# Scan's beginning for block 0, moved from the scan stage into the mixture's results

## What is computed

```python
# L1_ffn: two of 16 experts for each token, and a shared one
score = sigmoid(x @ gate_w + gate_b); top two, their scores scaled to a sum of 1
y = mlp(x, shared) + sum over the two of share * mlp(x, expert)   # mlp: (silu(x wg) * (x wu)) wd

# L2_attn: the scan
x, z = split(x @ in_proj)                  # 512 channels each
x = silu(causal_conv(x, 4 taps) + conv_b)
dt, B, C = split(x @ x_proj)               # 64, 16, 16
dt = softplus(dt @ dt_proj + dt_b)
h = exp(dt * A) * h + dt * B * x           # over time, for 512 channels x 16 states
y = (sum over states of h * C + D * x) * silu(z)
y = y @ out_proj
```

## Time and profile before

| | us |
|---|---|
| runs shown: median (lowest to highest, 3) | 4324.62 (4317.84 to 4327.66) |
| profiled execution | 4317.54 |
| its span | 4315.7 |
| PE busy | 3985.7 (92%) |
| DVE busy | 3321.2 (77%) |
| ACT busy | 2878.3 (67%) |
| POOL busy | 1998.7 (46%) |

### The profile page before, as it was taken

The page is one execution under the profiler, slowest core; times in us unless marked ns, Lnnn a source line. Parts: engine busy times, 40 slices in busy tenths (PEclk is TensorE's granted clock), DMA queues, the critical chain, the costliest instruction groups (busy, mean ns, idle before and its releaser), DMA issues. The chain is left out here.

```text
span 4315.7 us, 100840 instructions
## 1 busy us (share of the span) xinstructions
PE 3985.7 (92%) x39408; PEld 2128.4 (49%) x39417; DVE 3321.2 (77%) x5680; ACT 2878.3 (67%) x4588; POOL 1998.7 (46%) x1891
## 2 busy tenths in 40 slices
PE   8899999888959757899999999999999999999897
PEld 4344444565638423354544445455454555555555
DVE  7899999686665569888888888886137888888586
ACT  5577777664553465888888888875125777777664
POOL 6222222251335635888888888886001222222332
PEclk9899999999969878899999999999999999999999
DMA  5211111105235345455555555654223222222100
GB/s 148 64 39 39 40 40 40 27 28 131 66 119 159 99 113 123 124 155 160 149 169 147 149 146 156 171 149 136 87 90 106 67 64 62 61 70 61 31 13 27
DMA packets 263805, 412.40 MB, mean 96 GB/s; under 512 B 52731, under 2 KB 139802, under 8 KB 263170
## 3 DMA queue, kind: packets, MB, share of 16 engines
q1 hardware_dynamic: 228966, 375.81, 31.2%
q0 software_dynamic: 6912, 18.88, 1.7%
q10 hardware_dynamic: 27456, 11.28, 1.2%
HBM read 351.85 MB, written 53.24 MB: 94 GB/s over the span
## 5 line engine op out<-in xcount | busy, mean ns | idle before, releaser
L2984 POOL TENSOR_TENSOR l_dbx<-l_u,l_bc 128x1024 f32<-128x1024 f32 x256 | 603.4, 2358 | 251.9 <-DVE l_u L3494 83.2
L1169 DVE CUSTOM_DVE_ANT_0 banks<-banks,l3s_table 128x1024 f32<-128x1024 f32 x512 | 619.4, 1241 | 88.7 <-PE banks L1089 84.3
L1252 ACT ACTIVATE l3s_probs<-banks 128x512 f32<-128x512 f32 x1024 | 540.3, 595 | 203.7 <-PE banks L1118 100.4
L1164 DVE TENSOR_REDUCE l0s_peak<-banks 128x1 f32<-128x1024 f32 x512 | 605.3, 1214 | 58.4 <-PE banks L1089 58.0
L1252 ACT ACTIVATE l0s_probs<-banks 128x512 f32<-128x512 f32 x1024 | 535.6, 600 | 165.0 <-PE banks L1089 163.3
L3292 ACT ACTIVATE banks<-l_dt,l_decay 128x512 f32<-128x512 f32 x512 | 346.7, 687 | 223.1 <-DVE banks L3505 220.6
L2994 POOL TENSOR_TENSOR l_ys<-l_ys,l_hc 128x1024 f32<-128x1024 f32 x203 | 479.6, 2363 | 22.2 <-DVE l_hc L3516 22.0
L3166 PE MATMUL banks<-l_ha,l_ring 128*128 128x512 f32 x1024 | 446.6, 593 | 3.6 <-issue 3.6
L3166 PE MATMUL banks<-l_hb,l_ring 128*128 128x512 f32 x1024 | 443.1, 593 | 1.4 <-ACT l_hb L3257 0.9
L3505 DVE TENSOR_TENSOR_SCAN banks<-banks,l_carry,l_dbx 128x512 f32<-128x512 f32 x256 | 319.2, 1278 | 68.9 <-ACT banks L3292 62.0
L1089 PE MATMUL banks<-l3s_q_st,l3s_k_st 122*32 122x512 bf16 x4096 | 346.7, 381 | 4.9 <-ACT l3s_probs L1252 1.0
(11 more groups left out here) (535 smaller groups left out, 7201.7 us busy)
## 6 DMA issues: line engine op xcount, KB each, us to landing
l_bc<-l_bc_rows SPq DMA_DIRECT2D x256, 512.0 KB, 5.3
l_ring<-in_l2f_stream SPq DMA_DIRECT2D x176, 512.0 KB, 6.5
l3s_table<-bias_table SPq DMA_DIRECT2D x16, 960.0 KB
qk_parts<-l0s_probs SPq DMA_DIRECT2D x96, 128.0 KB, 2.4
qk_parts<-l3s_probs SPq DMA_DIRECT2D x32, 384.0 KB, 3.5
...
```

The costliest lines, as they stand in the source:

```text
L1164: nc.vector.tensor_reduce(out=peak[:, b % 2, t:t + 1], in_=s1[t % 2], axis=AX, op=ALU.max, negate=True).then_inc(s1_used, 1)
L1169: nc.vector.tensor_tensor_reduce(out=s1[t % 2], in0=s1[t % 2], in1=rows, scale=1.0, scalar=LOW, op0=ALU.add, op1=ALU.max, accum_out=peak[: ...
L1252: nc.scalar.activation(columns(probs[b % 2][:, t, :], half * 512, (half + 1) * 512), scores, ACT.Exp, scale=scale).then_inc(s2_used, 1)
L2984: nc.gpsimd.tensor_tensor(dbx[:, at:at + 2], u[:, 2 * mh:2 * mh + 2], bc[:, load % BR, 0].unsqueeze(1).to_broadcast([P, 2, TB]), ALU.mult)\
```

## The change

A new class `ScanHead` holds what both stages share. Its SBUF tensors outlive the mixture: `room` holds the mixture's `xt` and later the scan's xs, dt, zs and xc; `u` holds the mixture's `rows` and `out_b` and later the scan's u; `wo` holds the experts' down weights and later the four broadcast buffers `bc`. In the mixture the head's `w_x` and `w_dt` lie in `hot`, its `w_in` in experts 8 to 15 of `wo`, and its turned rows and softplus parts in the first three blocks of `acc`.

In the mixture the queues become:

- SP loads the head's small parameters ahead of the 80 stores, `w_in` behind them; behind that it waits for x_dbl, stores its B and C rows and loads the first broadcast.
- PE runs the shared expert for all eight blocks as far as its buffers allow, and then the head's turns, projections, x_dbl and the first two tiles of dt.
- ACT copies the shared expert's sum out of PSUM into `acc`, in place of DVE's reading it there. The head's steps stand between its post-norm rows.
- DVE makes four hidden rows first and two behind each of the sums 0 and 1; add(n-1) follows combine(n), and the shift of n-1 stands ahead of combine(n).
- POOL no longer makes the scan's norm; the power of the mixture's last block is its only other operation. The root of the head's norm is made on ACT.

```diff
+            head.load(sp)
             for b in range(BLOCKS):
                 sp.wait_ge(b_out, b + 1)
                 sp.dma_start(y_rows[b * P:(b + 1) * P, :], out_b[:, b % AHEAD, :]).then_inc(b_put[b % AHEAD], 16)
+            head.load_in(sp)
+            head.store(sp)
 
...
+            pe.wait_ge(out_used, NB)
+            head.tensor(pe)
...
+            def keep_shared(n):
+                act.wait_ge(out_ready, n + 1)
+                nc.scalar.copy(acc[:, n * BT:(n + 1) * BT, :], outs[n % 2]).then_inc(out_used, 1)
+                if n + 2 < NB:
+                    gate_rows(n + 2)
+
+            def post_rows(n):
+                if n < NB - 1:
+                    posts[n % 2].root(act, n // 2)
+                posts[n % 2].scalar(act, n // 2, lambda k: acc[:, n * BT + k, :], lambda k: acc[:, n * BT + k, :])\
+                    .then_inc(normed_ready, 1)
...
-            for n in range(NB):
-                if n + 2 < NB:
-                    gate_rows(n + 2)
-                wait(act, added, n - 1)
-                if n < NB - 1:
-                    posts[n % 2].root(act, n // 2)
-                posts[n % 2].scalar(act, n // 2, lambda k: acc[:, n * BT + k, :], lambda k: normed[:, n % 2, k, :])\
-                    .then_inc(normed_ready, 1)
+            for n in range(4):
+                keep_shared(n)
+            post_rows(0)
+            for n in range(4, 6):
+                keep_shared(n)
+            post_rows(1)
+            keep_shared(6)
+            keep_shared(7)
+            head.norm.root(act, 0)
+            head.decay_rates(act)
+            post_rows(2)
+            head.normalise(act)
+            head.keep_turned(act)
+            head.keep_x(act)
+            post_rows(3)
+            head.silu_z(act)
+            head.silu_x(act)
+            head.keep_dbl(act)
+            post_rows(4)
+            act.wait_ge(added, 3)
+            head.soften(act)
+            for n in range(5, NB):
+                post_rows(n)
```

```diff
             def combine(n):
+                v.wait_ge(out_used, n + 1)
                 v.wait_ge(got_ready[n % 4], 16 * CHOICES * BT * (n // 4 + 1))
-                v.wait_ge(out_ready, n + 1)
-                for c, (done, rows_of) in enumerate(((out_used, lambda k: outs[n % 2][:, k, :]),
-                                                     (summed, lambda k: acc[:, n * BT + k, :]))):
+                for c in range(CHOICES):
+                    v.drain()
                     for k in range(BT):
                         t = n * BT + k
                         last = nc.vector.scalar_tensor_tensor(
-                            out=acc[:, t, :], in0=got[:, n % 4, c, k, :], scalar=share[:, t, c:c + 1], in1=rows_of(k),
+                            out=acc[:, t, :], in0=got[:, n % 4, c, k, :], scalar=share[:, t, c:c + 1], in1=acc[:, t, :],
                             op0=ALU.mult, op1=ALU.add)
...
+                last.then_inc(summed, 1)
+                v.drain()
                 wait(v, normed_ready, n - 1)
                 posts[n % 2].statistics(v, lambda k: acc[:, n * BT + k, :])
 
             def add(n):
                 v.wait_ge(normed_ready, n + 1)
                 x = chip.x[:, n * BT:(n + 1) * BT, :]
-                nc.vector.tensor_tensor(x, x, normed[:, n % 2], ALU.add).then_inc(added, 1)
-
-            hidden_rows(0)
-            hidden_rows(1)
+                nc.vector.tensor_tensor(x, x, acc[:, n * BT:(n + 1) * BT, :], ALU.add).then_inc(added, 1)
...
+            for n in range(4):
+                hidden_rows(n)
             for n in range(NB):
-                if n == NB - 1:
-                    wait(v, added, 1)
-                    following.statistics(v, lambda k: chip.x[:, k, :])
-                combine(n)
                 if n:
                     posts[(n - 1) % 2].vector(v, (n - 1) // 2)
-                if n + 2 < NB:
-                    hidden_rows(n + 2)
-                if n >= 2:
-                    add(n - 2)
+                combine(n)
+                if n < 2:
+                    hidden_rows(2 * n + 4)
+                    hidden_rows(2 * n + 5)
+                if n:
+                    add(n - 1)
+                if n == 1:
+                    v.drain()
+                    head.statistics(v)
+                    head.clear(v)
+                if n == 2:
+                    head.norm.vector(v, 0)
+                if n == 3:
+                    head.convolve(v)
+                    head.negate(v)
+                if n == 6:
+                    head.step_size(v)
             posts[(NB - 1) % 2].vector(v, (NB - 1) // 2)
-            add(NB - 2)
             add(NB - 1)
 
...
             for n in range(NB):
-                if n == NB - 1:
-                    following.gpsimd(g, 0)
                 if n + 2 < NB:
                     results(n + 2)
             posts[(NB - 1) % 2].gpsimd(g, (NB - 1) // 2)
```

The head's steps on PE and ACT (the others, `convolve`, `step_size`, `soften`, have the same operations as those of the scan stage for half 0):

```diff
+    def load(self, sp):
+        a = self.a
+        for t, src in ((self.taps[:], a["taps"]), (self.conv_b[:], a["conv_b"]), (self.dt_b[:], a["dt_b"]),
+                       (self.decay[:], a["log"]), (self.w_x, a["w_x"].rearrange("(c p) n -> p c n", p=P)),
+                       (self.w_dt, a["w_dt"])):
+            sp.dma_start(t, src).then_inc(self.loaded, 16)
+
+    def load_in(self, sp):
+        sp.dma_start(self.w_in, self.a["w_in"].rearrange("(c p) n -> p c n", p=P)).then_inc(self.in_loaded, 16)
+
+    def store(self, sp):
+        sp.wait_ge(self.dbl_kept, 1)
+        sp.dma_start(self.bc_rows[0].rearrange("i s t -> (i s) t"), self.x_dbl[self.rank:self.rank + 2 * self.states, :])\
+            .then_inc(self.bc_stored, 16)
+        sp.wait_ge(self.bc_stored, 16)
+        row = bass.AP(tensor=self.bc_rows.tensor, offset=0, ap=[[0, P], [self.states * TB, 2], [1, TB]])
+        sp.dma_start(self.bc[:, 0], row).then_inc(self.bc_loaded[0], 16)
+        sp.wait_ge(self.bc_loaded[0], 16)
...
+        pe.wait_ge(self.rows_ready, 1)
+        for c in range(KC):
+            for k in range(BT):
+                last = nc.tensor.transpose(self.bank(self.TURNED[c])[:, k * P:(k + 1) * P],
+                                           self.rows[:, k, c * P:(c + 1) * P], self.chip.ident[:])
+            last.then_inc(self.turned, 1)
+        pe.wait_ge(self.in_loaded, 16)
+        pe.wait_ge(self.turned_kept, KC)
+        for half, filled in ((0, self.x_filled), (1, self.z_filled)):
+            for i in range(CT):
+                for c in range(KC):
+                    at = (half * CT + i) * P
+                    last = nc.tensor.matmul(self.bank((self.X, self.Z)[half][i]), self.w_in[:, c, at:at + P], self.xt[:, c, :],
+                                            start=(c == 0), stop=(c == KC - 1))
+                last.then_inc(filled, 1)
...
+        pe.wait_ge(self.z_kept, 1)
+        for i in range(CT):
+            pe.wait_ge(self.x_silu, i + 1)
+            last = nc.tensor.matmul(self.bank(self.DBL)[0:self.rank + 2 * self.states], self.w_x[:, i, :], self.xs[:, i, :],
+                                    start=(i == 0), stop=(i == CT - 1))
+        last.then_inc(self.dbl_filled, 1)
+        pe.wait_ge(self.dbl_kept, 1)
+        pe.wait_ge(self.z_kept, CT)
+        for i in range(2):
+            nc.tensor.matmul(self.bank(self.DT[i]), self.w_dt[:, i * P:(i + 1) * P], self.x_dbl[0:self.rank, :],
+                             start=True, stop=True).then_inc(self.dt_filled, 1)
...
+    def keep_x(self, act):
+        act.wait_ge(self.loaded, 16 * 6)
+        for i in range(self.CT):
+            act.wait_ge(self.x_filled, i + 1)
+            bank = self.bank(self.X[i])
+            self.nc.scalar.activation(self.xc[:, i, self.TAPS - 1:], bank, ACT.Copy)
+            self.nc.scalar.activation(bank, bank, ACT.Identity, scale=self.taps[:, i, self.TAPS - 1:self.TAPS],
+                                      bias=self.conv_b[:, i:i + 1]).then_inc(self.tap_done, 1)
```

```diff
+            sp.dma_start(w_dt[:], a["w_dt"]).then_inc(dt_loaded, 16)
+            for i in range(1, BR - 1):
+                bc_load(0, i)
+            sp.dma_start(w_in[:], a["w_in"].rearrange("(c p) n -> p c n", p=P)).then_inc(first_loaded, 16)
+            for t, src in ((w_x, a["w_x"].rearrange("(c p) n -> p c n", p=P)),
                            (w_out, a["w_out"].rearrange("(c p) n -> p c n", p=P)), (skip, a["skip"]),
                            (sc, m["scales"]),
                            (so, bass.AP(tensor=m["s3"].tensor, offset=0, ap=[[0, P], [1, D]]))):
...
             weights_to(WR)
-            bc_store(0)
-            sp.wait_ge(bc_stored, 16)
-            for i in range(BR - 1):
-                bc_load(0, i)
             for n in range(NB + 1):
...
-            nc.gpsimd.memset(xc[:, :, 0:TAPS - 1], 0.0).then_inc(xc_cleared, 1)
-
...
-            for c in range(KC):
-                turn_rows(0, c)
-            pe.wait_ge(first_loaded, 16 * 3)
-            for i in range(CT):
-                project_x(0, i)
-            for i in range(CT):
```

(31 more changed lines are left out.)

231 lines of the change are left out of this document (154 added, 77 removed).

## The result

The changed kernel takes 4329.07 us in the median (18 runs, 4323.65 to 4334.88), the kernel before 4321.09 (18 runs, 4316.24 to 4327.81). The ratio is 1.0018 with an interval of 1.0011 to 1.0025: 8.0 us more, forecast were 5.9 (as a time 4330.5, counted from the 4324.6 of the first three runs). It is a small loss, inside the 0.2% that the prediction called no change.

What follows compares the result with a forecast made beforehand. DVE and ACT, each waiting for the other, were taken to bound the mixture's results. 36.6 us more there, 38.3 less at the scan's start and 7.6 back from a late broadcast load gave +5.9: 4323.4 (or 4330.5), range 4313 to 4344.

Steps and rivals of the forecast that it cites:

- no change: Whole kernel: a trade that about cancels, within 0.2% (8.6 us); this was the forecast itself, chance 0.50.
- Results: Mixture's stage collecting its results: the scan's beginning lengthens the chain between DVE and ACT there, 36.6 us more.
- x_proj's half clock: PE at x_proj in the mixture: a pause lowers the clock, 1.7 us more, bounds 0 and 3.4.
- the 1.3 for overlap: Layout of the mixture's sums: 1.3 us taken off its end because neighbouring instructions overlap a little.
- the wait ahead of the power in the tail: POOL behind the mixture's last sum: its first power after the gathers waits 5.6 us, bounds 0 or 5.6.
- The scan's start: Start of the scan stage: first scan 3.3 us after the mixture's end instead of 41.6, 38.3 us saved.
- Load 3: Scan block 0: a broadcast load behind all weights in SP's queue delays pair 4 by 7.6 us, bounds 2 and 11.
- the diagonals: ACT's loop in the scan: 16 diagonals of 1.2 us each behind four exponentials; only one pause costs, 0.6 us.
- (b): Scan stage: clearly slower, a late broadcast row makes POOL and DVE wait 11 to 12 us; +11.5 us, chance 0.27.
- (c): Mixture and scan start: clearly faster, no power wait, x_proj at full clock, broadcast row in time; -7 us, chance 0.20.
- (d): Mixture's results: POOL's gathers run later and bound the stage; +10 us, chance 0.03.
- the signs named: Trace: mixture's end near 1561, sums 3 and 4 23 us apart, POOL waits, first scan 3 to 4 us in.

Runs made afterwards that it cites:

- the repeat of before: The kernel before, run again unchanged for a second trace; its whole execution took 4328.8 us.

## Why the prediction came out as it did

**Results, +36.6 forecast, +31.9 measured.** The laying-out held step by step. In us, forecast and measured:

| | sum 1 starts | 1 to 2 | 2 to 3 | 3 to 4 | 4 to 5 | 5 to 6 | 6 to 7 | tail |
|---|---|---|---|---|---|---|---|---|
| forecast | 1456.7 | 15.0 | 11.1 | 23.4 | 14.0 | 11.4 | 12.5 | 16.3 |
| measured | 1457.0 | 14.8 | 10.7 | 22.9 | 15.7 | 11.0 | 12.4 | 11.6 |

(The measured start is 1469.6 less the 12.6 us by which the whole stage is later.) The 1.7 too much at 4 to 5 is the term for x_proj's half clock, which the forecast had as a term of its own. Without the tail the forecast's sum, less the 1.3 for overlap and with the 1.7 for the clock, is right to 0.1 us; small errors of both signs cancel in it. The step that failed is the wait ahead of the power in the tail, taken at 5.6 and measured at 0.1. The tail came out 4.7 short and not 5.6, because the power itself took 1.94 us, where the mixture's power before took 1.03. It was the upper of its two bounds, chosen because "the row is of just this situation, a first power behind gathers". The situation was another: the row has an addition and a drain between gathers and power, and it is these that the change takes away. The prediction had named that as the lower bound. "GPSIMD Engine Reference", section "Instruction dispatch", of the Trainium skill has a freshly loaded Q7 kernel pay about 6 us once; the size and the once agree with 5.63, but by that page the first call would pay, and the first power (1562.82) did not stand.

**The scan's start, 38.3 forecast, 36.5 measured.** The first scan comes 5.1 us behind the mixture's end and not 3.3. It is the same 5.63 us, of which 1.55 come out here; with them paid ahead of the power it was 3.55. So one wrong reading cost the forecast 4.7 one way and 1.8 the other.

**Load 3, 7.6 forecast, 6.4 measured.** (The 0.6 that the prediction names for the diagonals is not in its sum.) The landing at 24 us after the stage's start (the product behind it began at 1593.18, 24.4 behind the mixture's end) and the wait of 10 us were right, and spreading the weights took 5.5 of the 6.4 away. Wrong was that load 3 alone was the cause: with it moved, load 4 held POOL for 8 us.

**The sum.** By its own steps +5.9, in the two traces +1.9, and against the repeat of before, which lies 2.0 us lower in the same three stretches, +3.9. Ahead of them the 80 expert blocks take 0.7 (means of all traces) to 1.3 us more (the first two traces), which the prediction held to be unchanged; six small loads stand on SP's queue ahead of the stores there, but I have no run on it. That makes about 3 to 5 of the 8.0 us. The rest lies in stretches that no step of the prediction had. In the means of three traces without and eleven with the change these are the attention, +6.9, the part of the kernel ahead of it, +1.3, and the part behind the step product, -3.3; that last part varies from 2722.8 to 2729.1 us without the change, so none of the three is firm. So the median came within 2.1 us of the forecast partly by luck: the forecast's own stretch came out 2 to 4 us under its +5.9, and stretches that it did not look at added 4 to 6.

**The rivals.** (b), slower by load 3, named a landing at 27 or later; the product behind it began at 24.4. (c) needed three things: the power without a wait came true, x_proj at full clock and load 3 in time did not. (d) did not occur; POOL waited 46 us for the last statistics. Of the signs named, the sums' distances, the broadcast wait at the fourth product and the end of the mixture (1556.1 on the old scale, near the 1555 "without POOL's wait") came as written; POOL's wait of 5 to 6 us ahead of its power and a first scan 3 to 4 us into the stage did not.

**Open.** Whether the change makes the windowed attention longer, and why. One trace each speaks against the places in SBUF and the order of the DRAM tensors; the places of semaphores and of the instruction stream in memory are not tried. And whether the drain itself is what waits.
